# Group norm, quantised grouped 1x1 convolution and residual, one core: a shorter statistics lead, a new prologue, a new end, and the Newton step moved from GpSimd to VectorE

## What is computed

```python
xg = x.reshape(B, G, Cg, H, W)[:, perm]                 # perm = 1, 2, 3, 0; x here is _gn(x)
xa = jnp.clip((xg - lA) / (uA - lA), 0.0, 1.0)
xa = ste_round(xa * (ACT_LEVELS - 1)) / (ACT_LEVELS - 1)
...
y = jnp.einsum('bgihw,goi->bgohw', xa, wg).reshape(B, C, H, W)
inv = gamma / jnp.sqrt(running_var + BN_EPS)
y = y * inv[None, :, None, None] + (beta - running_mean * inv)[None, :, None, None]
y = jax.nn.relu(y)
return y + identity
...
x = x + _L0_conv_ref(_gn(x), L0_conv_weight, ...)
```

## Time and profile before

| | us |
|---|---|
| median of 3 runs (264.43 to 264.54) | 264.53 |
| the profiled execution, its own time | 266.27 |
| its span, first to last instruction | 264.5 |

### The profile page before, as it was taken

One profiled execution on the slowest core, in us unless ns is written; L12 is line 12 of the kernel. 1 busy time (PEld: TensorE's weight loads), 2 busy tenths in 40 slices (PEclk: granted clock), 3 DMA queues, 4 the chain that ended last, 5 costly groups with the idle time before them and its releaser, 6 DMA issues.

```text
span 264.5 us, 4055 instructions
## 1 busy us (share of the span) xinstructions
PE 184.9 (70%) x997; PEld 103.7 (39%) x997; DVE 235.7 (89%) x359; ACT 204.7 (77%) x378; POOL 235.4 (89%) x383
## 2 busy tenths in 40 slices
PE   0024498677779797788868678978777797775870
PEld 0023455344445453444425244445443454432330
DVE  1476989999999999999999999999999999795790
ACT  2344699999898999899998989898989696908000
POOL 6395689999999999999999999999999999999940
PEclk9999999999979899988999997979999869999597
DMA  5999999999999999999999999999999999999468
GB/s 154 402 410 410 410 406 408 414 397 331 417 416 416 408 417 417 415 417 417 414 413 417 416 417 417 415 415 417 415 417 417 417 412 402 393 397 375 178 243 327
DMA packets 34614, 103.28 MB, mean 390 GB/s; under 512 B 1296, under 2 KB 1824, under 8 KB 34592
## 3 DMA queue, kind: packets, MB, share of 16 engines
q1 hardware_dynamic: 19632, 58.07, 55.7%
q10 hardware_dynamic: 14960, 44.97, 42.6%
HBM read 51.65 MB, written 51.38 MB: 389 GB/s over the span
## 4 chain that ended last, share of the span: by engine, by line
POOL 72%; issue 9%; DVE 5%; PE 5%; DMA 3%; ACT 2%; ACTq 1%; POOLq 1%; DVEq 0%; SPq 0%
POOL images L388 50%; POOL levels L397 7%; DMA images<-in_x 3%; PE prod L552 2%; POOL q_bias L378 2%; DVE stats L435 2%; PE var_ps L542 1%; ACT levels L251 1%; POOL newt L371 1%; DVE images L458 1%; POOL newt L372 1%; POOL rstd L373 1%; POOL dev L350 1%; POOL mean_rstd L374 1%; POOL dev L353 1%
## 5 line engine op out<-in xcount | busy, mean ns | idle before, releaser
L552 PE MATMUL prod<-codes,w_t 128*128 128x392 bf16 x768 | 156.2, 354 | 35.2 <-DVE images L458 21.0
L388 POOL TENSOR_SCALAR images<-images,y_scale,y_bias 128x784 f32<-128x784 f32 x128 | 147.7, 1167 | 0.0
L458 DVE SCALAR_TENSOR_TENSOR images<-prod,floor,images 128x784 f32<-128x784 f32 x128 | 126.9, 1016 | 3.0 <-PE prod L552 2.0
L552 PEld LDWEIGHTS prod<-codes,w_t 128*128 128x128 bf16 x768 | 73.7, 105 | 109.2 <-issue 54.6
L251 ACT ACTIVATE levels<-images,q_bias,q_scale 128x784 int16<-128x784 f32 x95 | 90.3, 1029 | 9.5 <-POOL y_bias L379 9.1
L435 DVE BATCH_NORM_STATS2 stats<-images 128x6 f32<-128x392 f32 x140 | 70.7, 551 | 11.0 <-DMA images<-in_x 11.0
L218 ACT ACTIVATE unused<-images 128x784 bf16<-128x784 f32 x58 | 49.2, 851 | 11.8 <-DMA images<-in_x 10.9
L224 ACT ACTIVATE unused<-images,sums 128x784 bf16<-128x784 f32 x58 | 54.6, 944 | 3.0 <-issue 2.8
L450 DVE TENSOR_SCALAR codes<-levels 128x3136 bf16<-128x3136 int16 x32 | 42.2, 1319 | 4.3 <-POOL levels L397 4.2
L397 POOL TENSOR_SCALAR levels<-images,q_scale,q_bias 128x784 int16<-128x784 f32 x33 | 32.9, 998 | 0.1
L542 PE MATMUL var_ps<-dev,avg 128*128 128x8 f32 x128 | 18.5, 271 | 13.6 <-POOL dev L357 13.6
(11 more groups left out here) (60 smaller groups left out, 84.9 us busy)
## 6 DMA issues: line engine op xcount, KB each, us to landing
images<-in_x SPq DMA_DIRECT2D x31, 1568.0 KB, 13.2
out<-images ACTq DMA_DIRECT2D x28, 1568.0 KB, 15.5
out<-images SPq DMA_DIRECT2D x3, 1568.0 KB, 5.5
images<-in_x SPq DMA_DIRECT2D x4, 392.0 KB, 6.1
out<-images SPq DMA_DIRECT2D x4, 392.0 KB, 5.5
w_raw<-in_weight SPq DMA_DIRECT2D x1, 256.0 KB, 7.6
rows<-in_channel_params ACTq DMA_DIRECT2D x1, 8.0 KB, 2.3
bounds<-in_limits ACTq DMA_DIRECT2D x1, 2.0 KB, 6.2
```

What stands on the lines that cost most here:

```text
L388: nc.gpsimd.tensor_scalar(here, here, y_scale[:, u % 2, j, o:o + 1], y_bias[:, u % 2, j, o:o + 1], ALU.mult, ALU.add).then_inc(y_ready, 1)
L458: nc.vector.scalar_tensor_tensor(out=two, in0=prod[:, k % SETS, :, 0:HALF], scalar=floor[:, o:o + 1], in1=two, op0=ALU.max, op1=ALU.add).t ...
L552: done = nc.tensor.matmul(prod[:, k % SETS, h, 0:HALF], w_t[:, part, output_group(g)], codes[:, n % 2, g, h * HALF:(h + 1) * HALF], start= ...
```

## The change

1. **Chain.** `AHEAD` is 5 instead of 6, and three groups of VectorE statistics are taken for the first two pairs, not three. TensorE formed the means of the pair of images n+4 and n+5 ahead of multiply(n+1,0) for even n; now it forms those of n+3 and n+4 there, for odd n. It averages the deviations right behind that multiply. ScalarE copies the mean behind the first of the three quantisings of n+2, then runs the other two, the statistics of n+5, and then the standard deviation. GpSimd runs the deviations behind its second affine, and the coefficients behind its first affine of the next image.
2. **Newton step.** `inverse_std` on VectorE: reciprocal, square, times minus half the variance, plus 1.5 times the reciprocal, each waiting for the one before. It stands behind finish(n,0) for even n. GpSimd's `coefficients` has three operations left, on wider tables (`norm`, `scaled`, `coef`).
3. **Prologue.** The limits come as one row of 16 bytes and are spread by a matmul into `cols`; image 1 is loaded in four pieces too; the weights are quantised on VectorE, between the statistics of images 0 and 1.
4. **End.** For the last four images (`HELPED`) ScalarE does two of the four affines; `ACT_STORES` is 30.

```diff
-AHEAD = 6
-ACT_STORES = 28
+AHEAD = 5
+SINGLE = 2
+HELPED = 4
+ACT_STORES = 30
...
+            def affine(n, g):
+                u, j, o = n // 2, n % 2, output_group(g)
+                act.wait_ge(q_act, q_act_until(n - 1) + o + 1)
+                here = images[:, n % RING, o]
+                nc.scalar.activation(here, here, ACT.Identity, bias=coef[:, u % 2, 1, 1, G * j + o:G * j + o + 1],
+                                     scale=coef[:, u % 2, 0, 1, G * j + o:G * j + o + 1]).then_inc(y_act, 1)
...
+            for n in range(-1, B - 1):
+                m = n + AHEAD
+                if n % 2:
+                    u = (n + 3) // 2
+                    for g in range(quant_on_act(n + 2) if n + 2 < B else 0):
+                        quantise(n + 2, g)
+                        if g == 0 and u < PAIRS:
+                            copy_mean(u)
+                    store(n - 1)
+                    if m < B:
+                        image_stats(m)
+                    if u < PAIRS:
+                        deviation(u)
+                    for g in range(G - affine_on_act(n + 1), G):
+                        affine(n + 1, g)
+                else:
+                    for g in range(G - affine_on_act(n + 1), G):
+                        affine(n + 1, g)
+                    if m < B:
+                        image_stats(m)
+                    store(n - 1)
+                    for g in range(quant_on_act(n + 2) if n + 2 < B else 0):
+                        quantise(n + 2, g)
...
-                linked(u, 1, nc.gpsimd.tensor_tensor(newt[:, 0], rough[:], rough[:], ALU.mult))
-                linked(u, 2, nc.gpsimd.tensor_tensor(newt[:, 1], newt[:, 0], half_var[:], ALU.mult))
-                linked(u, 3, nc.gpsimd.tensor_tensor(newt[:, 2], three_halves[:], newt[:, 1], ALU.subtract))
-                linked(u, 4, nc.gpsimd.tensor_tensor(rstd[:], newt[:, 2], rough[:], ALU.mult))
...
+                linked(u, 1, nc.gpsimd.tensor_tensor(norm[:, 1], gmean[:, par].rearrange("p j g -> p (j g)"), norm[:, 0],
+                                                     ALU.mult))
+                linked(u, 2, nc.gpsimd.tensor_tensor(scaled[:], norm[:].unsqueeze(2).to_broadcast([P, 2, 2, 2 * G]),
+                                                     coef_mul[:].unsqueeze(3).to_broadcast([P, 2, 2, 2 * G]), ALU.mult))
+                nc.gpsimd.tensor_tensor(coef[:, par], scaled[:], coef_add[:], ALU.add).then_inc(coef_done, 1)
...
-            for n in range(B - 1):
-                for g in range(G):
+            for n in range(-1, B - 1):
+                mine = G - affine_on_act(n + 1)
+                for g in range(mine):
                     affine(n + 1, g)
-                if n % 2 == 0 and n // 2 + 2 < PAIRS:
-                    deviations(n // 2 + 2)
+                    if n % 2 and g == 1 and (n + 3) // 2 < PAIRS:
+                        deviations((n + 3) // 2)
+                    if n % 2 == 0 and g == 0 and (n + 2) // 2 < PAIRS:
+                        coefficients((n + 2) // 2)
                 if n + 2 < B:
                     quantise(n + 2)
-                if n % 2 == 1 and (n + 3) // 2 < PAIRS:
-                    coefficients((n + 3) // 2)
...
+            def inverse_std(u):
                 dve.wait_ge(std_done, u + 1)
-                nc.vector.reciprocal(rough[:], std[:]).then_inc(rough_done, 1)
...
+                nc.vector.reciprocal(rough[:], std[:]).then_inc(newton_step, 1)
+                dve.wait_ge(newton_step, 3 * u + 1)
+                nc.vector.tensor_tensor(newt[:, 0], rough[:], rough[:], ALU.mult).then_inc(newton_step, 1)
+                dve.wait_ge(newton_step, 3 * u + 2)
+                nc.vector.scalar_tensor_tensor(out=newt[:, 1], in0=newt[:, 0], scalar=-1.0, in1=half_var[:],
+                                               op0=ALU.mult, op1=ALU.mult).then_inc(newton_step, 1)
+                dve.wait_ge(newton_step, 3 * u + 3)
+                nc.vector.scalar_tensor_tensor(out=norm[:, 0], in0=newt[:, 1], scalar=1.5, in1=rough[:],
+                                               op0=ALU.add, op1=ALU.mult).then_inc(rstd_done, 1)
...
                 finish(n, 0)
+                if n % 2 == 0 and (n + 2) // 2 < PAIRS:
+                    inverse_std((n + 2) // 2)
                 finish(n, 1)
...
-                if n % 2 == 1 and (n + 3) // 2 < PAIRS:
-                    rough_rstd((n + 3) // 2)
...
-            for n in range(B - 1):
-                chain = n % 2 == 0 and n // 2 + 2 < PAIRS
+            for n in range(-1, B - 1):
+                chain = n % 2 == 1 and (n + 3) // 2 < PAIRS
+                if chain and n > 0:
+                    average_means((n + 3) // 2)
+                multiply(n + 1, 0)
...
                 if chain:
-                    average_means(n // 2 + 2)
-                multiply(n + 1, 0)
+                    average_deviations((n + 3) // 2)
                 multiply(n + 1, 1)
                 multiply(n + 1, 2)
-                if chain:
-                    average_deviations(n // 2 + 2)
                 multiply(n + 1, 3)
```

208 lines of the change are left out of this document (97 added, 111 removed).

## The result

The changed kernel takes 273.73 us (median of 4 runs, 273.37 to 274.3), against 264.53 us: a ratio of 1.033 over all runs of both (a further run of the kernel before took 265.72), with a 95% interval from 1.0303 to 1.0356. It is slower by 9.2 us, where 9.0 had been forecast. The profiled execution took 273.45 us with a span of 271.7. Before it was 266.27 with 264.5, so the profiled span grew by 7.2 us.

What follows compares the result with a forecast made beforehand. GpSimd was taken to set the old pace narrowly, the loop through ScalarE the new one; 36.7 + 200.2 (13 loops) + 12.3 (last loop) + 17.95 + 6.35 (end) = 273.5 us, range 269.5 to 286.

Steps and rivals of the forecast that it cites:

- pair 1's reciprocal: Start of the run up to VectorE's reciprocal for the second pair of images, forecast at 36.7 us.
- The loop through ScalarE: Steady pairs: finish, multiply, means, ScalarE's quantisings, statistics and deviation, then reciprocal and Newton step; 15.35 us a pair instead of 14.19.
- VectorE alone needs 14.15: Steady pairs: VectorE's own work, 13.50 us without waiting plus 0.65 for the Newton step, is the floor of a pair.
- GpSimd's coefficients fall to 0.84: Steady pairs: nine coefficient operations of 2.32 us on GpSimd become three of 0.84 us.
- Image 1's last quarter lands no earlier: Prologue: image 1's load time was taken as unchanged, so VectorE's sums end at about 17.0 us.
- ScalarE's list bites for the first time: Before pair 1's reciprocal: two quantisings, four statistics and the deviation, 6.1 us, make VectorE wait about 6 us.
- The end: From pair 15's reciprocal: 17.95 us to VectorE's last finish, then an unchanged 6.35 us to the span's end.
- So I take the span as the time: Whole run: the forecast span of 273.5 us was used as the time, since the old span equalled the median.
- The cap of the odd image: Rival: in every loop this VectorE cap waits about 0.85 us for GpSimd's affine, 11 us in all, 284.5 us; chance 0.2.
- The Newton operations: Rival: VectorE's new operations wait for GpSimd's affines, 0 to 2.9 us a pair, up to 311 us; chance 0.06.
- The faster rival: Steady pairs: the deviation is ready in time, VectorE never waits, 14.15 us a pair, 257.3 us; chance 0.12.
- I leave them out: Whole run: transfers, 248 us for 103.28 MB, were ignored as bounding only a kernel faster by 6%.

Runs made afterwards that it cites:

- Experiment 1: The changed kernel with ScalarE making the standard deviation ahead of the four statistics of image n+5 instead of behind them; 261.24 us, ratio 0.985.
- experiment 2: The changed kernel with the Newton step back on GpSimd in four operations, VectorE keeping the reciprocal alone; 263.99 us, ratio 0.9954.
- experiment 9: The changed kernel without ScalarE's two affines for each of the last four images, GpSimd doing all four; 275.65 us, ratio 1.0396.
- Experiment 4: The changed kernel with two spare reciprocals, results unused, behind the Newton step on VectorE; 274.84 us, ratio 1.0375.
- experiment 3: The kernel before with only the Newton step moved from GpSimd to VectorE, five coefficient operations staying on GpSimd; 278.28 us, ratio 1.0496.

## Why the prediction came out right, step by step

| step | predicted | measured |
|---|---|---|
| pair 1's reciprocal | 36.7 | 35.15 |
| 13 loops to pair 14's | 200.2 | 199.08 |
| last loop | 12.3 | 12.21 |
| pair 15's reciprocal to VectorE's end | 17.95 | 17.6 |
| VectorE's end to the span's end | 6.35 | 7.66 |
| span | 273.5 | 271.7 |

- **The loop through ScalarE closes and sets the pace: right.** The forecast was 15.35 us, measured are 15.24, with VectorE idle for 1.08 (1.2), ScalarE for 2.08 before the mean (nearly 2) and 0.73 for the Newton step (0.75). Finish to mean copied took 1.69 (1.68), mean to reciprocal 5.92 (6.02). Experiment 1 shows the cause, experiment 2 the step's share of it. Two pairs were longer. The one of 15.88 has a mean granted clock of 0.79. The one of 15.53 stands at 1.00 throughout, and there a finish of VectorE starts 0.3 us late with no releaser named. Together they cost 0.9 us, where the allowance of 0.05 a pair gave 0.65.
- **VectorE alone needs 14.15: right.** Experiment 1 has 14.07.
- **GpSimd's coefficients fall to 0.84: right**, 127.50 to 128.33 is 0.83, and it brings nothing, since GpSimd waits 1.94 us right before.
- **The prologue: the right way, but the term of 36.7 was 1.55 us too long.** The failed step is "Image 1's last quarter lands no earlier": the sums stand at 14.95 instead of 17.0. Besides, the 512-wide operations on VectorE took 0.53 once and 0.43 three times, not 0.55. Half of the gain was lost again before the first reciprocal, which came 1.1 us ahead of the forecast. One place is where GpSimd's operation of 0.2 us meets VectorE's weights (timelines of GpSimd and VectorE):

```profile
17.06 0.74 POOL L366 TENSOR_TENSOR dev<-sums,gmean 128x8 f32<-128x8 f32 x1
```

```profile
17.04 0.69 DVE L523 TENSOR_TENSOR w_t<-w_rest,w_t 128x512 bf16<-128x512 f32 x1
```

The wait of 6 us before pair 1's reciprocal, "ScalarE's list bites for the first time", came and was 5.44.
- **The end: right to 0.35 us on VectorE, 1.3 us short behind it.** The last finish-to-end stretch was taken over unchanged and became longer. The two profiles of experiment 9 point to the new end itself: without ScalarE's affines the same stretch is 6.36.
- **"So I take the span as the time": wrong.** Every execution on record, of every kernel here, lies 1.7 to 2.0 us above its own span: 266.27 with 264.5, 273.45 with 271.7. The span before equalled the median only because the profiled execution was itself 1.7 us slower than the median. A span of 273.5 would have meant a time of 275.3. That the span was forecast 1.8 too long cancels it, so the nearness of 273.5 to 273.73 is partly luck. The lengths of the steps are not.
- **The rivals.** The cap of the odd image never waited: every one took 0.96 or 0.97, by a margin of 0.04 us at 128.29. Experiment 4 shows that the margin was wider than the records say, and experiment 3 what it costs where it is missed. The Newton operations never waited in the changed kernel's steady pairs, 0.17 us each, because GpSimd was idle there. Where GpSimd is in an affine they do wait: in experiment 1's first pair, VectorE has

```profile
33.40 0.17 DVE L484 SCALAR_TENSOR_TENSOR newt<-newt,half_var 128x8 f32<-128x8 f32 x1
33.60 0.77 DVE L487 SCALAR_TENSOR_TENSOR norm<-newt,rough 128x8 f32<-128x8 f32 x1
```

So a VectorE operation with two SBUF inputs waits for GpSimd as well as the reverse, which the rows of before didn't show. The Trainium skill, page "SBUF — State Buffer", section "Who interferes with whom", says that of the two whichever starts first keeps the port. By that rule the traces agree in both directions (0.70 for a cap, 0.60 for this operation); in a near tie the records' starts don't tell who was first (experiment 4).
- **The faster rival** ("the loop doesn't close", 257.3) was the right description of what experiment 1 builds, with nearly the same pace (14.15 against 14.07). Its price left out the bytes, which hold that kernel at 261. "I leave them out" was right for the forecast and wrong for that rival.

## What to carry to other kernels

When engines work down fixed lists, follow one item of work around all of them, back to the place where it began. If the sum of that ring is longer than each engine's own work, the ring is the pace, and every small operation put between two of its steps costs its full length in every turn, however idle the engine that it relieves. The signature in the profile is that no engine is full and each waits once a turn for another one. The cure is to move the step of the ring ahead of work that doesn't belong to it, here the deviation ahead of the statistics (12.5 us), and then to look at once for what comes next: VectorE's own work, a second ring, TensorE's clock, the bytes.

## What the runs showed of the hardware

- Time in which an operation is kept from the port counts as its own: caps of 0.97 us show as 1.56 to 1.70 busy, small ones of 0.17 as 0.77. A busy share close to one can hold waiting.
- A cap whose record starts 0.08 us behind that of an affine still wasn't held up (experiment 4), while one that starts 0.12 behind was the earlier trace rows; in the same kernel another, also 0.12 behind, wasn't (46.99, 0.96 us long, beside an affine whose record starts at 46.87).
- In the one run with a broadcast of a 16-byte row to 128 partitions in the first microseconds, all transfers ran at 197 GB/s from 6 to 8 us, against 309 to 359 in ten kernels without it, and the first chain was some 0.9 us later than their mean.
- A wait of 0.85 us put into TensorE's list once in each pair went with a mean granted clock of 0.81 instead of 0.97. A lower clock need not lengthen a pair: in experiment 1 two at 0.88 take the same 14.07 us as those at 1.00.
- The time of an execution lies 1.7 to 2.0 us above its own span, in all executions on record, of fourteen kernels. So a profile's span is compared with the time of that same execution, not with the median of others.
